# A perceiver kernel on one core: which engine normalises the third block of tokens ahead of the feed-forward, and where fourteen idle transposes stand

## The reference

```
x = x + L0_xattn(layernorm(x), ctx)      x = x + L1_xattn(layernorm(x), ctx, masks)
x = x + L0_attn(layernorm(x))            x = x + L1_attn(layernorm(x))
x = x + L0_ffn(layernorm(x))             x = x + L1_ffn(layernorm(x))
```

```
y  = s4d(x ...) * (1 + gate * scale_out) + gate * shift_out   # the end of the mixing
xt = x_text + y
h  = layernorm(xt, g_ffn, b_ffn)          # the norm that the change is about
h  = gelu(h @ W1 + b1) @ W2 + b2          # the feed-forward, 512 -> 2048 -> 512
xt = xt + h
return layernorm(xt, g_norm_out, b_norm_out)

layernorm(x, g, b) = (x - mean(x)) * rsqrt(var(x) + 1e-5) * g + b   # over the 512 features
```

## Time and profile before

| | |
|---|---|
| runs of before | 1803.25, 1791.06, 1805.01 us (median 1803.25) |
| the profiled execution | 1802.59 us, its span 1800.8 us |
| TensorE, matmuls | 1675.6 us busy, 93% of the span |
| VectorE | 993.6 us, 55% |
| ScalarE | 595.0 us, 33% |
| GpSimd | 359.1 us, 20% |
| mean granted clock of TensorE | 0.949 of full speed |

### The profile page before, as it was taken

One profiled execution on the slowest core, in us unless ns is written; L12 is line 12 of the kernel. 1 busy time (PEld: TensorE's weight loads), 2 busy tenths in 40 slices (PEclk: granted clock), 3 DMA queues, 4 the chain that ended last, 5 costly groups with the idle time before them and its releaser, 6 DMA issues. The chain is left out here.

```text
span 1800.8 us, 23403 instructions
## 1 busy us (share of the span) xinstructions
PE 1675.6 (93%) x8886; PEld 1304.1 (72%) x8886; DVE 993.6 (55%) x1525; ACT 595.0 (33%) x1085; POOL 359.1 (20%) x327
## 2 busy tenths in 40 slices
PE   7799999999998989998999998989599899999996
PEld 4799999999995777864565656668486666676772
DVE  1569678687684634456999996653525630000014
ACT  4353454444521211103544432154245521111110
POOL 0521331233121020011554542300200010000010
PEclk9899999999999989998998988989798989999998
DMA  4322131323113567548163552220001097696860
GB/s 132 110 78 88 56 110 61 98 62 111 55 42 124 193 251 267 183 147 295 60 228 115 174 212 94 94 112 1 18 32 48 12 325 262 220 337 228 301 221 30
DMA packets 113044, 251.45 MB, mean 140 GB/s; under 512 B 14726, under 2 KB 44438, under 8 KB 108182
## 3 DMA queue, kind: packets, MB, share of 16 engines
q1 hardware_dynamic: 104352, 230.72, 36.8%
q10 hardware_dynamic: 6006, 10.62, 1.7%
q0 software_dynamic: 2560, 8.39, 1.4%
HBM read 230.95 MB, written 18.75 MB: 139 GB/s over the span
## 5 line engine op out<-in xcount | busy, mean ns | idle before, releaser
L415 PE MATMUL x_s_ps<-x_cxt,x_qs 128*128 128x400 f32 (+1 forms) x1152 | 246.1, 359 | 9.5 <-POOL x_qs L388 5.5
L1204 PEld LDWEIGHTS e_ps<-e_xg,e_w 128*128 128x128 f32 x1792 | 209.8, 195 | 35.7 <-issue 35.5
L441 PE MATMUL x_o_ps<-x_cx,x_pt 128*128 128x386 f32 (+1 forms) x1248 | 230.3, 343 | 0.0
L441 PEld LDWEIGHTS x_o_ps<-x_cx,x_pt 128*128 128x128 f32 (+1 forms) x1248 | 220.6, 190 | 1.4
L1204 PE MATMUL e_ps<-e_xg,e_w 128*128 128x128 f32 x1792 | 212.8, 279 | 9.0 <-issue 6.1
L415 PEld LDWEIGHTS x_s_ps<-x_cxt,x_qs 128*128 128x128 f32 x1152 | 207.3, 192 | 10.8 <-issue 10.6
L1196 PE MATMUL e_ps<-e_w,xt 128*128 128x512 f32 x352 | 163.2, 606 | 3.7 <-DMA e_w<-in_L_ffn_W 3.7
L2398 PE MATMUL x_s_ps<-x_cxt,x_qs 128*128 128x512 f32 (+1 forms) x384 | 140.7, 523 | 2.8 <-ACT x_sc L2519 1.7
L1443 DVE TENSOR_TENSOR e_y<-e_ps,e_b 128x512 f32<-128x512 f32 x20 | 13.7, 687 | 210.2 <-PE e_ps L1196 210.2
L491 DVE TENSOR_TENSOR x_pt<-x_t_ps,x_pt 128x512 fp32r<-128x512 f32 (+1 forms) x128 | 74.7, 586 | 92.3 <-ACT x_pt L581 92.1
L2398 PEld LDWEIGHTS x_s_ps<-x_cxt,x_qs 128*128 128x128 f32 x384 | 67.9, 194 | 79.3 <-issue 78.5
(11 more groups left out here) (437 smaller groups left out, 2736.6 us busy)
## 6 DMA issues: line engine op xcount, KB each, us to landing
e_w<-in_L_ffn_W SPq DMA_DIRECT2D x16, 4096.0 KB, 16.5
x_cxt<-in_ctxT SPq DMA_DIRECT2D x8, 2401.5 KB, 8.8
x_cx<-in_ctx SPq DMA_DIRECT2D x8, 2304.0 KB
e_w<-in_L_ffn_gate_up_proj SPq DMA_DIRECT2D x8, 2048.0 KB, 8.5
x_stage<-in_ctxT SPq DMA_DIRECT2D x16, 768.0 KB, 4.4
x_stage<-in_ctx SPq DMA_DIRECT2D x16, 768.0 KB, 6.2
e_w<-in_L_ffn_down_proj SPq DMA_DIRECT2D x8, 1024.0 KB, 9.4
x<-in_ctxT SPq DMA_DIRECT2D x8, 768.0 KB, 4.4
```

Of the source, the lines that this page charges most:

```text
L415: last = nc.tensor.matmul(s_ps[:, n, 0:b - a], qs[:, u % 2, p, c, :], cxt[:, q, c, a:b], start=(m + c == 0), stop=(m + c == len(PARTS) + C ...
L441: last = nc.tensor.matmul(o_ps[:, 0:WIDE], pt[0:rows, p, t, :], cx[0:rows, q, t, :], start=(t + m == 0), stop=(t + m == KT - 1 + len(PARTS ...
L1204: last = nc.tensor.matmul(u_ps[:, g % 2, a * PER + n, :], w1[:, e % PAIR, m, a * hidden + c * P:a * hidden + (c + 1) * P], xg[:, m, :], st ...
```

## The change

`by_act` goes from 3 to 2 (the last argument of `Centred`), so block 2 goes VectorE's way as block 3 does. In the feed-forward, VectorE does the statistics of blocks 2 and 3, then the rows of blocks 2 and 3, and only then `first_low(0)`. ScalarE's total, squares and row of block 2 and GpSimd's minus mean of it go. `stats` and `mv` have an entry per block now and lie inside `junk`, which no one writes in this stage any more. The 14 idle transposes move from ahead of block 3's transposes to the end of TensorE's list in `mixing`, behind `back(3)`.

```diff
-            norm = Centred(core, aside, "n5", y, xn, TT - 1)
+            norm = Centred(core, aside, "n5", y, xn, 2)
...
-        self.stats = core.sb(ctx, f"{name}_stats", [P, 6], side="right")
-        self.mv = core.sb(ctx, f"{name}_mv", [P, 2], side="right")
+        self.stats = self.junk[:, 0:TT * 6].rearrange("p (t n) -> p t n", n=6)
+        self.mv = self.junk[:, TT * 6:TT * 8].rearrange("p (t n) -> p t n", n=2)
...
-            pool.wait_ge(self.mv_ready, 1)
-            G.tensor_scalar_add(self.var[:, one], self.mv[:, 1:2], EPS).then_inc(self.var_ready, 1)
+            pool.wait_ge(self.mv_ready, t - self.by_act + 1)
+            G.tensor_scalar_add(self.var[:, one], self.mv[:, t, 1:2], EPS).then_inc(self.var_ready, 1)
...
+    def statistics(self, dve, t):
+        dve.wait_ge(self.src_ready, t + 1)
+        self.core.nc.vector.bn_stats(self.stats[:, t, :], self.src[:, t, :]).then_inc(self.stats_ready, 1)
+        dve.wait_ge(self.stats_ready, t - self.by_act + 1)
+        self.core.nc.vector.bn_aggr(self.mv[:, t, :], self.stats[:, t, :]).then_inc(self.mv_ready, 1)
+
+    def row(self, dve, t):
+        dve.wait_ge(self.rstd_ready, t + 1)
+        dve.wait_ge(self.mv_ready, t - self.by_act + 1)
+        self.core.nc.vector.tensor_scalar(self.normed[:, t, :], self.src[:, t, :], self.mv[:, t, 0:1], self.rstd[:, t:t + 1],
                                           ALU.subtract, ALU.mult).then_inc(self.last_ready, 1)
...
@@ mixing, tensor
                     back(t)
+                for n in range(IDLE):
+                    nc.tensor.transpose(ps[:, 0, (n % KC) * P:(n % KC + 1) * P], core.ident[:, :], core.ident[:, :])
@@ feed_forward, gpsimd
-                norm.pool_minus(pool, TT - 2)
                 norm.pool_rstd(pool, TT - 2)
                 norm.pool_rstd(pool, TT - 1)
@@ feed_forward, tensor
                 for t in range(TT):
-                    if t == TT - 1:
-                        for n in range(IDLE):
-                            nc.tensor.transpose(tps[:, t, n % KC, :], ident[:, :], ident[:, :])
                     norm.wait(pe, t)
@@ feed_forward, scalar
                 norm.act_rows(act, 1)
-                norm.act_total(act, TT - 2)
...
                 first_high(0)
-                norm.act_squares(act, TT - 2)
                 first_high(1)
-                norm.act_rows(act, TT - 2)
@@ feed_forward, vector
-                norm.last_statistics(dve)
+                for t in range(norm.by_act, TT):
+                    norm.statistics(dve, t)
+                for t in range(norm.by_act, TT):
+                    norm.row(dve, t)
                 dve.wait_ge(forward.w1_in, 64)
                 first_low(0)
-                norm.last_row(dve)
                 first_low(1)
```

More of the change, by code:

```diff
@@ L2915, in wait @@
         else:
-            engine.wait_ge(self.last_ready, 1)
+            engine.wait_ge(self.last_ready, t - self.by_act + 1)
 def mixing(core, forward, xs, y, spec_k, mix, scale, late, norm):
```

## The result

The changed kernel took 1782.16 us, the median of 20 executions (1778.08 to 1802.66), against 1792.45 us of the kernel before, again over 20 (1784.36 to 1806.04). The ratio is 0.9953 with a 95% interval of 0.9931 to 0.9974: faster by half a percent, between 4.7 and 12.4 us, where 3.9 us were forecast. The time forecast, 1799.3 us, stood on a median of three executions, 1803.25 us, which was 10.8 us above that of twenty.

The account below looks back on a forecast made before the run. The prediction took ScalarE's block 2 and the idle transposes, in series before `up(0)`, as the bound. Its terms, 4.85 - 0 - 0.21 - 0.7 = 3.9 us, taken from 1803.25, gave 1799.3 us, range 1788 to 1806 us.

Parts of the forecast that it names:

- The bound: Between mixing and `up(0)`: one serial way, ScalarE's block 2 and the idle transposes, with VectorE and TensorE waiting in it.
- VectorE's new way: Feed-forward start: VectorE does rows 2 and 3 from 1175.53, so `x_value(0)` starts 4.85 us earlier, at 1180.75.
- The new last thing: Ahead of `x_value(0)`: VectorE's three subtractions end last and hide the transposes, which end 0.6 us before.
- The meeting: All engines at the mixing's end: moved idle transposes end at most 0.2 us behind VectorE; cost taken as 0.
- The rival with 1.5 us: Mixing's end: idle transposes hold up the meeting, feed-forward starts 1.5 us later; time 1800.9 us, chance 0.12.
- GpSimd beside VectorE: Inverse deviations of blocks 2 and 3: GpSimd slows beside VectorE's row 2, cost 0.21 us, between 0 and 1.1.
- The clock: TensorE, transposes and `up(0)`: low clock from about 1178 to 1187.8, 0.7 us given back, between 0 and 1.4.
- The level: Whole kernel: starting time taken from the profiled execution's 1802.59 us and the median before, 1803.25 us.
- the lower execution: Whole kernel: rival that the median falls in the lower group of runs, 1787.2 us with no cause in the change; chance 0.15.
- The range: Whole kernel's time after the change: 1788 to 1806 us.
- Chances: Whole kernel, with about 1% or 18 us as threshold: faster 0.03, same 0.95, slower 0.02.
- The rivals that were slower or not effective: Low clock lasting into the feed-forward, 1807 us, chance 0.07; change not doing what it says, 1802 us, chance 0.08.

Follow-up runs that it names:

- e3: Changed kernel with the 14 idle transposes back ahead of block 3's, leaving the norm change alone; first statistics to `down(0)` 15.92 us, ratio to before 1.0013.
- e4: Kernel of before with only the 14 idle transposes moved behind `back(3)`; first statistics to `down(0)` 16.43 us, ratio to before 0.9956.
- e7: Changed kernel with `first_low(1)` and `second_low(0)` moved behind the last `x_low`; first statistics to `down(0)` 13.44 us, ratio to before 0.9953.
- e6: Changed kernel with 28 idle transposes instead of 14 at the mixing's end, one execution; first statistics 2.02 us behind VectorE's last addition.
- e5: Changed kernel without any of the 14 idle transposes; first statistics to `down(0)` 15.13 us, ratio to before 0.9986.
- e11: Kernel of before, unchanged, timed against itself; `down(0)` 8.4 us behind the start of `up(0)`, ratio 0.9999.
- e15: Kernel of before, unchanged, timed against itself once more; ratio 1.001 (0.9984 to 1.0037).
- e10: Changed kernel, unchanged, timed again against the kernel of before; ratio 0.9939 (0.9906 to 0.9973).
- e14: Changed kernel without any of the 14 idle transposes, once more; first statistics to `down(0)` 14.31 us, ratio to before 0.9962.
- e1: Kernel of before, unchanged, timed against itself and profiled again; ratio 1.0 (0.9962 to 1.0039).
- e2: Changed kernel, unchanged, timed against the kernel of before and profiled again; ratio 0.9956 (0.9921 to 0.9991).
- e13: Kernel of before with only the 14 idle transposes moved behind `back(3)`, once more; first statistics to `down(0)` 17.48 us, ratio to before 0.9989.

## Why the prediction was right or wrong

**The bound: right.** ScalarE's way of block 2 and the idle transposes in series were the bound. e3 takes away the first alone and gains 3.3 us, e4 the second alone and gains 2.6 us with the meeting counted. Both together gain 4.5 and not 5.9, because VectorE's subtractions then end last; e7, which moves two of them, comes to 5.6.

**VectorE's new way: right to 0.1 us.** Row 2 was put at 1.99 us behind the first statistics and came at 1.98; row 3 at 2.95 and came at 2.99; `x_value(0)` at 5.22 and came at 5.26, a gain of 4.81 where 4.85 was worked out. The new last thing was named (three subtractions), and e7 shows it.

**The meeting: taken as 0, it cost 0.17 us.** The estimate of the transposes' end, 0.2 us behind VectorE at the latest, was the right number; it should have been kept, as e6 shows that the meeting waits for them. The rival with 1.5 us didn't happen, since the clock was high.

**GpSimd beside VectorE: 0.1 us of the 0.21.** The second power took 0.66 us against 0.56, beside row 2, and no first step was slow. The cost is below what the median of other norms gave. The text said that before's trace had no inverse deviation of this norm beside a busy VectorE; it had one, of an earlier block in the mixing, beside VectorE's L2962 from 1172.08 to 1172.77. GpSimd's timeline of before:

```profile
1172.26 0.58 POOL L2889 TENSOR_TENSOR n_rstd<-n_var,n_half 128x1 f32<-128x1 f32 x1 [0.15 <-POOL n_var L2883]
```

It took 0.58 us, 0.02 above the others. The Trainium skill's rule (GPSIMD Engine Reference, Key points) names VectorE instructions in a 2-port mode or with two SBUF inputs; the longer power lies beside row 2, with 0.10 us, but no run here shows in which mode row 2 ran, so the cause stays open.

**The clock: the mis-sized term.** The step "I expect the low clock from about 1178 until ... about 1187.8" and its 0.7 us given back failed. In after the clock was high until `up(0)` had begun, low for 3.4 us, and `up(0)` to `down(0)` took 7.71 us against 7.55: 0.16 given back. What the step left out is the idle transposes' own effect in their new place: with them the clock was high through the transposes in eight profiles of eight, without them there it was low in those of block 2 in four of four. The course that the text described came where they are gone: in e5 the way from `x_value(0)` to `down(0)` took 9.88 us against before's 9.16, 0.7 given back. One of its arguments was misread, too: film's matmuls did not bring the clock up in about 3 us. They run back to back from 1110.52, and TensorE by one stretch of before still has the low clock there:

```profile
1112.00:1116.00 4.00, 4.00 (x11) 0.50 1.00 422
```

In e11 and e15, executions that the prediction had no profile of, the kernel of before lost another 1.1 to 1.5 us in the stretch, and the changed one in e10 0.5. The sum of the terms as measured is 4.8 - 0.17 - 0.16 = 4.5 us for the first pair and 4.9 in the mean, not 3.9. On transposes and the clock, before's rise during them stands against the rule of the Trainium skill that was cited (TensorE: Matmul & The Clock Gate, Part 4: PE-mode transpose). For the time of the changed kernel the idle transposes at the mixing's end are of no use that shows: e5 and e14 do as well without.

**The level: wrong, and the largest part of the miss.** The step was "against the profiled execution's 1802.59 us" and the median of three. Both stood on the upper part of a spread of some 22 us. The text had the lower execution as a rival with 0.15, at 1787.2; it was the likely case. Of the 17.1 us between 1799.3 and 1782.16, 10.8 are the level; the other 6.4 are the gain, as the medians of twenty lie 10.3 us apart and 3.9 were forecast. The range ended at 1788, 5.8 us above the result: with the level of twenty and the forecast gain the time would have been 1788.6, just inside, so it took both to leave it.

**The whole gain: larger than the sum.** The first comparison, -8.4 us by its ratio, is over twice the forecast. The pooled -7.6 us (1.0) leaves 2.7 us over the profiles' 4.9. The stages behind show none of it in the profiles, and the code ahead of the mixing is the same. That executions of after had less of the low clock ahead of the mixing by chance fits the five profiles of each: 1168.0 us to the first statistics in the mean against 1174.0, of which, summed over stretches of 15 us, about 85 us were at the low clock against 93. But five of each with such a spread don't show it, and e6 and e7, whose code up to the mixing's end is the changed kernel's but for e6's 14 more idle transposes, came to 1183.3 and 1177.6 us. This stays open.

**Chances.** Within 1% of the kernel of before timed beside it, as 0.95 said. But the time itself is under the 1785 us that no case of the text reached, 21.1 us below the 1803.25 from which it counted. The rivals that were slower or not effective did not happen.

## What to carry to other kernels

Follow the chain backwards through every engine that waits in it: two serial pieces, a norm on one engine and filler work on another, were worth more together (4.5 us) than either alone (3.3 and 2.6), though less than their sum, because another engine came last. The sum from rows of single operations held to 0.1 us for VectorE's way, not for the clock. Filler on TensorE counts at the next meeting of the engines, so it should end before the last of the others does. And where untouched stages spread by 20 us, take the level from many executions and compare the stretch of the change itself, profile against profile, before looking for a second cause in the whole.

## What was not expected of the hardware

Unbroken matmuls ran 17.0 us at the low clock in one execution (872.90 to 889.90 in e1), and in another (e2) the clock was high from 876.50 on; the same 52 of them took 10.78 us and 5.86. Two executions of the same code thus differ by several us in a stage with no wait changed. Fourteen idle transposes at the mixing's end went with the high clock in the transposes of blocks 2 and 3, which begin 2.9 us behind the last idle one in after (eight profiles of eight); where block 2's come 6.0 us behind it, in e4 and e13, the eight took 1.99 us and not 1.31. The meeting of the engines comes 0.30 us behind the end of TensorE's last work and 0.32 behind VectorE's, as e6 and before show.
